# Attention heads of two layers: query parts stored once and read twice, first batches loaded in other places

## What is computed

```python
NH = 16                                   # heads, each of HD = 128 / 16 = 8 features
c_q = x @ W_dq;  Q = (c_q @ W_uq)         # layer 2; K and V from x @ W_dkv
scores = einsum('bqhd,bkhd->bhqk', Q, K) / sqrt(8)
scores = where(causal, scores, -inf)
out = einsum('bhqk,bkhd->bqhd', softmax(scores), V) ; x = x + out @ W_o

qkv = x @ wi.T + bi                       # layer 3, the same without the mask
o = softmax(heads(q) @ heads(k).T / sqrt(8)) @ heads(v) ; attn_out = o @ wo.T + bo
```

## Time and profile before

| | us |
|---|---|
| median of 3 runs | 3242.28 |
| lowest and highest | 3238.45 and 3243.86 |
| the profiled execution | 3245.29 |
| its span, from first to last instruction | 3243.2 |
| mean granted TensorE clock | 0.91 of 2.4 GHz |

### The profile page before, as it was taken

The page is one execution under the profiler, slowest core; times in us unless marked ns, Lnnn a source line. Parts: engine busy times, 40 slices in busy tenths (PEclk is TensorE's granted clock), DMA queues, the critical chain, the costliest instruction groups (busy, mean ns, idle before and its releaser), DMA issues. The chain is left out here.

```text
span 3243.2 us, 69838 instructions
## 1 busy us (share of the span) xinstructions
PE 2553.1 (79%) x20225; PEld 1822.0 (56%) x20225; DVE 2129.7 (66%) x4755; ACT 1631.4 (50%) x3623; POOL 764.2 (24%) x1097
## 2 busy tenths in 40 slices
PE   4657859989988786999459999997676999984191
PEld 2334543449877533999237777767443666653180
DVE  5967875237778633777756666657876888855086
ACT  1646513332254443667535666652553777764063
POOL 0000100000000176555432222200251222211670
PEclk7889979999999898999779999998888999997595
DMA  3095100111190211222594566500086566521133
GB/s 104 0 213 143 46 13 20 35 43 49 36 172 0 78 53 51 71 69 67 171 243 53 72 72 70 69 6 1 1 263 68 72 72 72 72 25 45 52 100 111
DMA packets 316152, 241.10 MB, mean 74 GB/s; under 512 B 27069, under 2 KB 297837, under 8 KB 315693
## 3 DMA queue, kind: packets, MB, share of 16 engines
q1 hardware_dynamic: 288248, 202.91, 31.6%
q0 software_dynamic: 19072, 28.28, 3.0%
q10 hardware_dynamic: 8704, 8.39, 0.9%
HBM read 139.83 MB, written 96.51 MB: 73 GB/s over the span
## 5 line engine op out<-in xcount | busy, mean ns | idle before, releaser
L2619 ACT ACTIVATE h_pt<-h_ps 128x384 f32<-128x384 f32 (+1 forms) x1024 | 543.5, 545 | 278.1 <-PE h_ps L2528 143.5
L2365 DVE TENSOR_REDUCE h_nm<-h_ps 128x4 f32<-128x1024 f32 (+1 forms) x448 | 539.2, 1218 | 153.9 <-PE h_ps L2499 62.3
L1900 POOL DMA_INDIRECT results<-e_y,e_ykey x208 | 217.0, 1043 | 162.6 <-DVE e_y L1889 143.5
L1857 DVE TENSOR_SCALAR e_wt<-w 128x1156 f32 (+1 forms) x208 | 141.2, 680 | 166.1 <-PEq L1626 87.7
L2547 PE MATMUL h_ps_o<-h_pt,h_vp 128*32 128x256 f32 (+1 forms) x4096 | 246.8, 358 | 1.3 <-ACT h_pt L2619 1.3
L1947 ACT ACTIVATE e_hid<-e_ps_h,e_wt 128x128 f32<-128x128 f32 x688 | 201.3, 369 | 13.4 <-PE e_ps_h L1921 8.8
L2533 PE MATMUL h_ps<-h_sq,h_sk 128*128 128x256 bf16 x1024 | 193.4, 275 | 9.2 <-ACT h_pt L2619 4.3
L1929 PE MATMUL e_ps_o<-e_wt,e_hid 128*128 128x128 f32 x1376 | 192.4, 279 | 4.8 <-DVE e_y L1889 4.8
L1921 PE MATMUL e_ps_h<-e_hT,e_wt 128*128 128x128 f32 x1376 | 195.1, 281 | 0.6 <-ACT e_hT L1942 0.3
L2470 PE MATMUL h_ps<-h_sk,h_sq 128*128 128x256 bf16 x1024 | 156.1, 276 | 42.6 <-DVE h_identb L2347 36.6
L1704 POOL DMA_INDIRECT sorted_rows<-e_row,e_pos x128 | 124.6, 974 | 256.2 <-DVE e_row L1682 218.3
(11 more groups left out here) (457 smaller groups left out, 6249.7 us busy)
## 6 DMA issues: line engine op xcount, KB each, us to landing
h_sk<-k_stack SPq DMA_DIRECT2D x192, 128.0 KB
q_stack<-p_parts SPq DMA_DIRECT2D x64, 256.0 KB, 3.0
h_sq<-q_stack SPq DMA_DIRECT2D x64, 256.0 KB
sorted_rows<-pad SPq DMA_DIRECT2D x26, 520.0 KB, 10.6
e_xt<-sorted_rows SPq DMA_DIRECT2D x104, 130.0 KB, 2.2
e_got<-results SPq DMA_DIRECT2D x24, 512.0 KB, 4.7
k_stack<-p_parts SPq DMA_DIRECT2D x32, 384.0 KB, 3.0
b_tz<-ktab SPq DMA_DIRECT2D x32, 256.0 KB, 7.1
```

The source lines that it names most:

```text
L1857: dve.tensor_scalar(wt[j % 4][:, :], w[:, :, :].rearrange("p e w -> p (e w)")[:, ds(at, wc)], 1.0, None, ALU.mult).then_inc(e_w.sem, 1)
L1900: gp.indirect_dma_start(ys[:, :], bass.IndirectOffsetOnAxis(ap=key[m // 4][:, m % 4:m % 4 + 1], axis=0), y[m][:, :], None).then_inc(return ...
L2365: dve.tensor_reduce(to, got, AX, ALU.max, negate=True).then_inc(s["mx"].sem, 1)
L2619: act.activation(pt[g % 2][:, j, :], ps_2[:, h % 2, 0:SW], ACT.Exp, scale=scale).then_inc(s["ex"].sem, 1)
```

## The change

- **Store.** q is stored in three planes, as k is: one DMA of 384 KB in place of three with 640 KB. `PARTS` is 2 x 16.
- **Load.** Rows 0 to 31 of `sq` come from the planes 0 and 1, each read twice: two DMAs of 16 rows, whose source is the 8 rows of a plane with a broadcast dimension of 2 in front (`rows.to_broadcast([2, HD, NH, SEQ])`). Each row still has 16 pieces of 256 tokens, 512 bytes. A load is six DMAs and the clearing one: `HEAD_LOADS` is 7. In the instruction the source is the list of dimensions (2 with stride 0, 128 with stride 8192, 256 with stride 1), the target is (16, 16, 256).
- **Where the first batches are loaded.** Batch 0 is loaded in the middle of the projection, behind the store of step n = 5 (`NU // 3`). Batch 1 is loaded behind the last store, with no wait of its own on the last stores. Batches 2 and 3 are loaded in the attention's block, behind the four loads of values; batch 3 waits there for the maxima of batch 0 (`maxima_in` at 48). SP's loop over the 16 steps is written out.
- **Start of the attention.** POOL, not DVE, sets the zeros and ones of `vp`. PE waits for `chained` in step b = -1 and no more at the start. PE's wait for the load of batch 3 goes from the first scores of batch 2 to the end of step 0.
- **End of the projection.** PE computes ten products of 128 x 384 that nothing reads (`dense_products`).

```diff
@@ -34,7 +34,7 @@
 CREDIT = 256
-HEAD_LOADS = 6
+HEAD_LOADS = 7
 HI, MID, LOW = 1, (0, 2), (2, 0)
@@ -212,6 +212,7 @@
         maxima_in = {t: sem(f"{t}_maxima_in") for t in ("h2", "h3")}
+        vp_set = {t: sem(f"{t}_vp_set") for t in ("h2", "h3")}
         first_v = {t: sem(f"{t}_first_v") for t in ("h2", "h3")}
@@ -313,7 +314,7 @@
                                                ("mid", 2), ("lo", 1), ("lo_gp", last), ("v", 1), ("vc", 1))},
-            stored=[SlotSignal(pool, f"{t}_stored{j}", 64, j, 3) for j in range(3)],
+            stored=[SlotSignal(pool, f"{t}_stored{j}", 32, j, 3) for j in range(3)],
             v_stored=[SlotSignal(pool, f"{t}_v_stored{j}", 16, j, 3) for j in range(3)])) for t, last in (("p2", 2), ("p3", 1))}
@@ -2052,7 +2053,7 @@
             d.rearrange("h e a t -> (h e a t)")[0:n * D * NB * SEQ].rearrange("(a p t) -> a p t", a=n, p=P)
-            for d, n in ((q_stack, 5), (k_stack, 3)))
+            for d, n in ((q_stack, 3), (k_stack, 3)))
         stw = ExitStack()
@@ -2109,7 +2110,7 @@
                 S = 3
-                PARTS = 4 * 16
+                PARTS = 2 * 16
                 nrm = [sb(f"{tag}_nrm{j}", [P, UT, P], stack=st) for j in range(S)]
@@ -2197,6 +2198,7 @@
                         staggered(pe, NU, S, (2, project), (1, turn), (2, project_v))
+                        dense_products(pe, ps_t, 10, P + SEQ)
 
@@ -2227,10 +2229,7 @@
                             sp.wait_ge(*(s["lo_gp"].now(n, 1) if 0 in on_gp else s["lo"].now(n, 1)))
-                            for a in range(2):
-                                sp.dma_start(q_to[:, 2 * a:2 * a + 2, :], parts[j][:, 0, a:a + 1, :].to_broadcast([P, 2, U])
-                                             ).then_inc(s["stored"][j].sem, 16)
-                            sp.dma_start(q_to[:, 4, :], parts[j][:, 0, 2, :]).then_inc(s["stored"][j].sem, 16)
+                            sp.dma_start(q_to, parts[j][:, 0, :, :]).then_inc(s["stored"][j].sem, 16)
                             sp.wait_ge(*s["lo_gp"].now(n, on_gp.index(1) + 1))
@@ -2242,13 +2241,17 @@
                                 sp.dma_start(buffers["sk"][u][KR:KM, :, :], ones_rows).then_inc(ones_in, 16)
-                        staggered(sp, NU, S, (0, store))
-                        for j in range(SLOTS * SEQ // U):
-                            sp.wait_ge(*s["stored"][j].now(0, PARTS))
-                            sp.wait_ge(*s["v_stored"][j].now(0, 16))
-                        for u in range(SLOTS):
+
+                        def load_first(u):
+                            sp.wait_ge(*s["stored"][0].now(0, PARTS))
                             load(sp, u, u, first_in[tag.replace("p", "h")][u])
                             clear_maxima(sp, u, first_in[tag.replace("p", "h")][u])
+
+                        for n in range(NU):
+                            store(n, n % S, n // S)
+                            if n == NU // 3:
+                                load_first(0)
+                        load_first(1)
                         for j in range(S):
@@ -2317,7 +2320,7 @@
                 with pool.loop_block(NB) as block:
-                    k_set = n_chain[0] + 8
+                    k_set = n_chain[0] + 2
 
@@ -2335,14 +2338,15 @@
                             load_values(b, b, first_v[tag])
+                        for b in range(2, SLOTS):
+                            if b == 3:
+                                sp.wait_ge(maxima_in[tag], 48)
+                            load(sp, b, b, first_in[tag][b])
+                            clear_maxima(sp, b, first_in[tag][b])
                         run(sp, step)
...
                     def _(dve):
-                        for n in range(2):
-                            link(dve, dve.memset(vp[n][:, :, :, :], 0.0))
-                            for half in range(2):
-                                link(dve, dve.memset(vp[n][:, :, half:NH:2, 16 * half + HD:16 * half + HD + 1], 1.0))
                         link(dve, dve.memset(zero[:, :], 0.0))
@@ -2403,6 +2407,12 @@
                     def _(gp):
+                        for n in range(2):
+                            gp.memset(vp[n][:, :, :, :], 0.0).then_inc(vp_set[tag], 1)
+                            gp.wait_ge(vp_set[tag], 3 * n + 1)
+                            for half in range(2):
+                                gp.memset(vp[n][:, :, half:NH:2, 16 * half + HD:16 * half + HD + 1], 1.0).then_inc(vp_set[tag], 1)
+                        gp.wait_ge(vp_set[tag], 6)
                         gp.wait_ge(chained, k_set)
@@ -2449,15 +2459,12 @@
                     def _(pe):
-                        pe.wait_ge(chained, k_set)
                         pe.wait_ge(ones_in, 16 * SLOTS)
...
                                 pe.wait_ge(first_in[tag][u], 16 * HEAD_LOADS)
-                                if b == 2:
-                                    pe.wait_ge(first_in[tag][3], 16 * HEAD_LOADS)
                             elif k == 0:
@@ -2577,6 +2584,8 @@
                         def step(b, u, r, first, turn, body, tail):
+                            if isinstance(b, int) and b == -1:
+                                pe.wait_ge(chained, k_set)
                             later = ahead(u, r, 2)
@@ -2606,6 +2615,8 @@
                                     max_scores(b + 2, *later, h)
+                            if isinstance(b, int) and b == 0:
+                                pe.wait_ge(first_in[tag][3], 16 * HEAD_LOADS)
 
@@ -2654,10 +2665,12 @@
             two = 2 * HD
-            sp.dma_start(heads_in["sq"][u][0:2 * two, :, :], q_rows[0:2 * two]).then_inc(up, 16)
+            for part in range(2):
+                rows = q_parts.rearrange("a (e h) t -> a e h t", h=NH)[part:part + 1, :, :, cols]
+                sp.dma_start(heads_in["sq"][u][part * two:(part + 1) * two, :, :], rows.to_broadcast([2, HD, NH, SEQ])).then_inc(up, 16)
             for n, part in ((0, 1), (1, 1), (2, 0)):
                 sp.dma_start(heads_in["sk"][u][n * two:(n + 1) * two, :, :], k_rows[part * HD:part * HD + two]).then_inc(up, 16)
-            sp.dma_start(heads_in["sq"][u][2 * two:KR, :, :], q_rows[3 * HD:5 * HD]).then_inc(up, 16)
+            sp.dma_start(heads_in["sq"][u][2 * two:KR, :, :], q_rows[HD:3 * HD]).then_inc(up, 16)
```

## The result

The changed kernel takes **3572.4 us** (median; 3570.2 to 3574.2), against 3243.1 us of the kernel before on the same chip: 1.101 times the time, 95% interval 1.100 to 1.103, some 329 us slower. The forecast was 3371, within 3225 to 3490: the direction was right, and the time lies 82 us above the range.

The account below looks back on a forecast made before the run. PE was taken to bound the attention, DVE, ACT and DMA the projection, with idle pauses between. Late loads +154.0 and heads -25.6 gave +128.4: 3373.7 from the profiled 3245.3, or 3371 by the median; range 3225 to 3490.

Parts of the forecast that it names:

- the load was put at 14.0 us: Each attention load on two engines: 14.0 us from issue, bounds 11.4 and 26.2, against a need of 11.5 and 11.0.
- The heads of the attentions: Start of both attentions: 24.0 and 26.5 us saved, less delays of 7.1, 8.1, 6.4 and 3.3; net -25.6 us.
- a dimension of 2 in front is two engines: Loads of rows 0 to 31: a transfer keeps to as many engines as its outermost dimension has entries, here two.
- Rival C: Loads use all 16 engines, none is late: about 3197 us (3185 to 3210); chance 0.10.
- the loss to the other 14 engines: Within a load, the two engines are slowed while the other 14 write: at most 2.6 us, taken as 1.6.
- 154 us: Attention steps: loads late by 2.5 us in h2 and 3.0 in h3, 28 times each, +154 us.
- rival D: Attention steps: A, and PE's clock falls in each wait, +70 to +137 us, 3441 to 3508; chance 0.13.
- A: The forecast itself: two engines, a load of 12 to 15 us, time 3371 (3259 to 3427); chance 0.64.
- ACT's stall in mid-projection: Batch 0's load delays the stores of step 6, so ACT's buffer is 7.1 us late, 8.1 in p3.
- The pause: Between POOL's last part of q and k and PE's first scores: 7.4 us in place of 31.4 and 33.9.
- The wait for batch 2: Early in each attention, batch 2 loads behind batch 1 and the values: PE waits 6.4 us in h2, 3.3 in h3.

Follow-up runs that it names:

- five planes: The changed kernel with the store and load of before put back (five planes of q stored, one load of 32 rows): 3208.7 us, ratio 0.989.

## Why the prediction was right or wrong

The way of the change was foreseen, for the reason given: two engines carry a third of the load and make it late. The time lies outside the range because two steps failed that add up: the load was put at 14.0 us and took 15.8 to 15.9, and the clock, kept as a rival of the forecast, was left out of its sum. The heads of the attentions were too hopeful besides.

**Right: a dimension of 2 in front is two engines.** The step was argued from three-row transfers on three engines. The windows of the changed kernel show a share of 0.07 to 0.15 for it, exactly 12 of 96 packets of the maxima come late, and the kernel before with that edit alone loses 385 us. The Trainium skill ("DMA: Bandwidth & Descriptors", Rules for kernel authors) says of a leading broadcast of c copies that it confines the DMA to c engines at most; the trace agrees, with 36 to 38 GB/s at a share of 0.15, as two engines would have it. Rival C, that all 16 would share, is out for this form of the load; for other forms (five planes, 3208.7 us) the 3197 given for it (its own sum is 3195.6) was 12 us too low.

**Wrong in size: 14.0 us for the load.** It was 15.8 and 15.9. Two terms of the sum were too small. The first: it let the two engines move a row each 30 ns from 1.3 us on. In the first two microseconds of data they had 19 GB/s or less, half of what two engines move later, while SP's issue of the two DMAs took 2.1 us: about 1 us, an estimate from these rows; that the slow issue is the reason was not tested. The second: the loss to the other 14 engines was put at 1.6 us, between 0 and 2.6. It was assumed that the others need 4.5 us; they were busy at some 113 GB/s for about five, and what is left of the 1.8 or 1.9 us, somewhat under 1, is put down to that. The run with 8 rows in front agrees that a row costs more than 30 ns where many engines write one tile. Late by 4.3 and 4.9 us, the loads cost 28 x (4.3 + 4.9) = 257 us in place of 154: **103 us** more.

**Wrong: the clock.** The forecast had this as its rival D, with 0.13, priced at 70 to 137 us. Its argument against was that waits of 2.5 to 3.0 us are shorter than the 4.4 after which the clock was seen low. That argument failed. In the step shown there are two waits in a row, 1.55 us for the maxima and 2.66 for the load with 0.4 us of work between them, and behind them the clock is at 0.50; in the run with the broadcasts last a single wait of 2.34 us was enough. What decides in which step the clock falls stays open. The stretch from first use to next issue grew by 1.25 and 1.3 us on average in h2 and h3, 28 x (1.25 + 1.3) = **71 us**, and keeping PE busy gave 83 back. A and D were not rivals: D came on top of A, and the sum put it at nothing.

**Not seen: the maxima.** They go through all 16 engines, 16 rows each, and the two busy engines hold back their share, the 12 packets of 96 above. PE waits for them 59 times, 101 us in all. Had the load been in time, this would have been a loss of its own; as it is, the load lands later still, and the wait can show only in the clock. The run with the broadcasts last takes it away and is 99 us faster (half of it by the earlier load), although PE's waits for the load are longer.

**The sum.** Between first and last matmul for the maxima the two attentions grew by 347.6 us. The 56 steps have 331.5 of them, where 154 were forecast; by the averages, lateness and clock are 257 + 71 = 328. The other 16.1 lie in the first steps, before SP issues the load of batch 4. With 18 us at the heads (below, the 16.1 among them) this leads from the forecast to 3371 + 177.5 + 18 = 3567, and 3572 were measured.

**The heads of the attentions: too hopeful by 18 us.** The forecast of -25.6 is -35.3 up to the starts of the attentions and +9.7 behind them. Measured are -23.4 and, in the first steps, +16.1: together -7.3. ACT's stall in mid-projection was 7.7 in p2, as forecast (7.1), and 11.7 in p3, where 8.1 were forecast with 2.0 us credited for stores. The pause is not 7.4 but 12.7 and 14.0 us, and SP's issues for batch 1 took 10 us, not 5: the three of `sk` alone are issued in 4.8. In the run with five planes, without a broadcast in the load, the same issues took 4.7 in all and the first pause was 10.5. The lines of POOL's last part, SP's issues and PE's start in the changed kernel:

```profile
1670.02 2.39 POOL L2173 TENSOR_TENSOR p_parts<-p_rest,p_parts 128x512 bf16<-128x512 f32 x2 [0.41 <-ACT p_parts L2223]
...
1674.03 3.16 SPq L2670 DMA_DIRECT2D h_sq<-q_stack  x2
1677.23 4.79 SPq L2672 DMA_DIRECT2D h_sk<-k_stack  x3
...
1685.06 0.58 PE L2489 MATMUL h_ps<-h_sk,h_sq 128*128 128x256 bf16 x2 [8.94 <-PEq L166]
```

```profile
2585.40 1.16 POOL L2173 TENSOR_TENSOR p_parts<-p_rest,p_parts 128x512 bf16<-128x512 f32 x1 [1.97 <-ACT p_parts L2223]
...
2600.54 1.87 PE L2477 MATMUL h_ps<-h_sk,h_sq 128*128 128x256 bf16 x8 [10.01 <-PEq L166]
```

The wait for batch 2 (forecast 6.4 and 3.3) did not come as a wait of its own; PE waited 5.1 us for the maxima of batch 0 at the start of h2 instead. That the dense products cost nothing was right; POOL's memsets and the moved waits were in the run with five planes, which was faster, and were not tested alone.

**The range** stopped at 3490 since it held A or D. With A's excess of 103 us or D's 71 to 83 alone it would have held; with both it did not.

## What to carry to other kernels

Look at the outermost dimension of each side of a DMA before anything else: a broadcast of 2 in front saved 256 KB of stores in each step of the projection and made each load last 16 us where 11 were to be had; reading a plane twice by two transfers with 16 rows in front cost no wait. When a transfer of a pipeline becomes late, add what the waiting does, too: another queue's small transfers that need all 16 engines are held as well, and waits of 2 to 3 us can bring TensorE's clock down, so that its price comes on top of the wait and is no alternative to it. And do not price a load by its best window: neither 30 nor 71 ns a row gave its time here.

## What the runs showed of the hardware

- The issue of a DMA on SP can take longer behind others: the three of `sk` take 1.88 us before, 5.15 behind two broadcast ones and 1.97 behind four of 8 rows. That SP waits there for the two engines is an inference from this.
- A wait of 1.55 and one of 2.66 us, with 0.4 us of matmuls between, were followed by a clock of 0.50 for some 3 us; one wait of 1.6 us in a step (8 rows in front, first attention) left it at 1.00. A single wait of 2.34 us was followed by 0.52, and one of 3.20 by 1.00 (the broadcasts last).
- Three transfers of POOL's queue over 16 engines, of 8 KB each, let PE go on only 10 us after their first issue (1922.78 to 1932.81), since 12 of their 96 packets moved between 1928 and 1932, the other 84 before 1926. The row of their issues:

```profile
1922.78 1.49 POOL L2455 DMA_DIRECT2D h_sq<-h_mT  x3 [2.33 <-ACT h_mT L2647]
```
